# Routed experts moved ahead in layers 1 and 3 of a four-layer mixture kernel: sends over two stages, gathers beside other work

## The reference

```python
x = L0_attn_src
xn = _layernorm(x); s = _L0_attn_ref(xn, ...); g = _silu(_L0_ffn_ref(xn, ...)); x = x + s * g
xn = _layernorm(x); s = _L1_attn_ref(xn, ...); g = _silu(_L1_ffn_ref(xn, ...)); x = x + s * g
xn = _layernorm(x); s = _L2_attn_ref(xn, ...); g = _silu(_L2_ffn_ref(xn, ...)); x = x + s * g
xn = _layernorm(x); s = _L3_attn_ref(xn, ...); g = _silu(_L3_ffn_ref(xn, ...)); x = x + s * g
```

## Time and profile before

| what | value |
|---|---|
| median of three runs | 4465.07 us |
| lowest and highest | 4442.44 and 4473.7 us |
| the profiled execution's own time | 4474.3 us |
| its span, first to last instruction | 4472.5 us |
| busy in the span: PE, DVE, ACT, POOL | 3023.8, 2326.8, 1525.0, 813.9 us |
| mean granted TensorE clock | 0.822 |
| bytes moved by DMA | 150.88 MB, mean 34 GB/s |

### The profile page before, as it was taken

How to read it: one execution, slowest core, us unless ns; L and a number is a source line. 1 busy time by engine, 2 the same in 40 slices (tenths; PEclk the granted TensorE clock), 3 DMA queues, 4 the chain that set the end, 5 groups by cost and what they waited for, 6 DMA issues and landing times. The chain is left out here.

```text
span 4472.5 us, 65620 instructions
## 1 busy us (share of the span) xinstructions
PE 3023.8 (68%) x22266; PEld 2082.8 (47%) x22266; DVE 2326.8 (52%) x5222; ACT 1525.0 (34%) x2598; POOL 813.9 (18%) x800
## 2 busy tenths in 40 slices
PE   6999526999932314794346299999881537599990
PEld 4555414777720313442145145555571325476790
DVE  5555663111145463499553488888534468412443
ACT  4444112333322000000222188888531332243340
POOL 0000000000018301200134350000025564000015
PEclk9999757999956556897678599999995768699995
DMA  2000000000000022000034110000151000000471
GB/s 102 1 1 0 1 8 10 5 9 9 5 6 29 6 38 39 1 0 0 4 102 145 37 39 1 1 1 1 55 181 37 31 7 1 11 10 4 140 213 60
DMA packets 124861, 150.88 MB, mean 34 GB/s; under 512 B 50012, under 2 KB 95593, under 8 KB 124041
## 3 DMA queue, kind: packets, MB, share of 16 engines
q1 hardware_dynamic: 106584, 107.60, 8.7%
q0 software_dynamic: 18096, 41.06, 2.9%
HBM read 108.23 MB, written 40.37 MB: 33 GB/s over the span
## 5 line engine op out<-in xcount | busy, mean ns | idle before, releaser
L2183 DVE CUSTOM_DVE_ANT_0 decayed_sd<-decayed_sc,decayed_decay 128x512 f32<-128x512 f32 x512 | 331.7, 686 | 86.2 <-PE decayed_sc L2060 86.0
L2138 ACT ACTIVATE decayed_pr<-decayed_sd,decayed_shift 128x512 f32<-128x512 f32 x512 | 338.9, 713 | 49.5 <-DVE decayed_shift L2190 49.3
L668 PEld LDWEIGHTS experts_down<-experts_w,experts_h 128*128 128x128 f32 x2048 | 263.9, 192 | 107.1 <-issue 103.5
L2072 PEld LDWEIGHTS decayed_tr<-all_ident,decayed_pr 128*128 128x128 f32 x2048 | 223.5, 141 | 175.5 <-ACT decayed_pr L2138 101.7
L2072 PE MATMUL decayed_tr<-all_ident,decayed_pr 128*128 128x128 f32 x2048 | 276.9, 278 | 11.0 <-ACT decayed_pt L2145 10.8
L736 DVE SCALAR_TENSOR_TENSOR L0c_G<-experts_down,all_gate,L0c_G 128x128 f32 x256 | 85.5, 351 | 371.1 <-PE experts_down L668 371.1
L441 PE MATMUL experts_up<-experts_xt,experts_w 128*128 128x256 f32 x1140 | 272.0, 386 | 0.0
L702 ACT ACTIVATE experts_h<-experts_up,experts_w 128x512 f32<-128x512 f32 x256 | 175.9, 687 | 281.1 <-PE experts_up L657 279.7
L668 PE MATMUL experts_down<-experts_w,experts_h 128*128 128x128 f32 x2048 | 264.7, 275 | 0.0
L657 PE MATMUL experts_up<-all_XNT,experts_w 128*128 x512 | 258.7, 597 | 5.3 <-DMA experts_w<-in_L_experts 5.3
L198 PE MATMUL norm_turned<-all_ident,norm_xn 128*128 128x128 f32 x128 | 35.7, 434 | 299.6 <-DVE norm_xn L136 299.6
(11 more groups left out here) (468 smaller groups left out, 6377.1 us busy)
## 6 DMA issues: line engine op xcount, KB each, us to landing
experts_w<-in_L_experts SPq DMA_DIRECT2D x78, 384.0 KB, 3.4
experts_w<-in_L_experts SPq DMA_DIRECT2D x43, 579.0 KB, 4.0
experts_tok<-rows_in SPq DMA_DIRECT2D x121, 128.0 KB, 3.4
rows_out<-experts_y POOLq DMA_DIRECT2D x121, 128.0 KB, 3.4
rows_in<-linear_zero SPq DMA_DIRECT2D x43, 128.0 KB, 1.8
experts_w<-in_L_experts SPq DMA_DIRECT2D x8, 514.0 KB, 3.4
experts_b<-in_L_experts_b SPq DMA_DIRECT2D x43, 64.0 KB, 4.2
moe_w<-in_L_moe SPq DMA_DIRECT2D x4, 514.0 KB, 3.5
```

Source lines behind the costliest of these rows:

```text
L668: last = pe.matmul(down[b % 2][:, t * P:(t + 1) * P], h[:, b % 2, f, t * P:(t + 1) * P], w2, start=(f == 0 and t == 0), stop=(f == nf - 1) ...
L2072: last = pe.transpose(tr[u % TURNED][:, t * P:(t + 1) * P], pr[:, u % RING, t * P:(t + 1) * P], m.ident[:, :])
L2138: act.activation(pr[:, u % RING, :], sd[:, u % RING, :], ACT.Exp, bias=shift[:, u % RING:u % RING + 1]).then_inc(exp_ready, 1)
L2183: dve.tensor_tensor_reduce(out=sd[:, u % RING, :], in0=sc[h][:, :], in1=decay[:, qt, :], scale=1.0, scalar=-3.0e38, op0=ALU.mult, op1=ALU. ...
```

## The change

In layer 1 the sends of tiles 0 to 17 stay in the short convolution, and those of tiles 18 to 31 are issued in part b of the solve, which ends GpSimd's stream with the wait for all of them. `m.T` is no longer a spare buffer, since it must live longer; the solve gets a buffer of its own, which ends with the scan. Routed experts 1 run right after the scan. Their 64 gathers are issued by GpSimd in the statistics phase, where ScalarE now squares in place; the mix of branches uses `m.XNT` as its spare. The mix of layer 1 starts without gathers of its own.

In layer 3 `conv_project_phase` issues 3 tiles of sends per block in place of 4 and no longer waits for them; `rotate_phase` issues the last 8 tiles, one per block, its loop on GpSimd being written out, and waits for all. Routed experts 3 run right after the gated output projection. Their gathers are issued in the soft mixture `moe3`. Layer 2 keeps its order and its gathers.

```diff
@@ expert_phase(..., pool_beside=None)
+        @block.gpsimd
+        def _(pool):
+            if pool_beside is not None:
+                pool_beside(pool)
@@
+def gather_rows(pool, m, rows, collected):
+
+    for n in range(NB):
+        for t in range(n * TPB, (n + 1) * TPB):
+            for k in range(2):
+                pool.indirect_dma_start(rows[k][:, t, :], None, m.rows_out, bass.IndirectOffsetOnAxis(m.SLOT[:, k, t:t + 1], 0)).then_inc(collected[n], 16)
@@ collect_mix_phase
-            for n in range(NB):
-                for t in range(n * TPB, (n + 1) * TPB):
-                    for k in range(2):
-                        pool.indirect_dma_start(...)
+            if gather:
+                gather_rows(pool, m, rows, collected)
@@ short_conv_phase, and the same stream added to part b of solve_phase
-            for t in range(NT):
-                send_tile(pool, m, t, sent)
-            pool.wait_ge(sent, 2 * NT * 16)
+            send(pool)
@@ branch_stats_phase
+        squared = centred
+
+        @block.gpsimd
+        def _(pool):
+            gather(pool)
@@ conv_project_phase
-                for t in range(n * TPB, (n + 1) * TPB):
+                for t in range(n * 3, n * 3 + 3):
                     send_tile(pool, m, t, sent)
-            pool.wait_ge(sent, 2 * NT * 16)
@@ rotate_phase
-            with pool.Fori(0, NB) as n:
+            for n in range(NB):
                 pool.wait_ge(r_ready, n + 1)
                 pool.tensor_tensor(half[2][:, :, :, :], side(n, 0), spread(sin), ALU.mult)
                 pool.tensor_tensor(half[3][:, :, :, :], side(n, 1), spread(cos), ALU.mult).then_inc(mult, 1)
+                send_tile(pool, m, 3 * NB + n, sent)
+            pool.wait_ge(sent, 2 * NT * 16)
@@ build_layers, layer 1
+            def send1(first, end):
+                def issue(pool):
+                    for t in range(first, end):
+                        send_tile(pool, m, t, sent1)
+                    if end == NT:
+                        pool.wait_ge(sent1, 2 * NT * 16)
+                return issue
-            short_conv_phase(nc, "conv", m, d, b[0:3], sent1)
+            short_conv_phase(nc, "conv", m, d, b[0:3], send1(0, 18))
-            solve_phase(nc, "solve", m, k, beta, b[5], solved)
-            delta_scan_phase(nc, "scan", m, q, k, kc, vc, solved, beta, flat_s)
+            with Scope(nc, "L1solved") as inner:
+                solved = inner.sb("solved", [P, NT * P])
+                solve_phase(nc, "solve", m, k, beta, b[5], solved, send1(18, NT))
+                delta_scan_phase(nc, "scan", m, q, k, kc, vc, solved, beta, flat_s)
+            routed_phase(nc, "experts1", ...)
             fir_phase(nc, "fir", m, d, vc, b[2], (b[0], b[5]), b[1], b[3])
+            rows1 = (m.T, a.sb("rows", [P, NT, P]))
-            branch_stats_phase(nc, "stats", m, branches, b[5], b[6], b[0], b[2])
+            branch_stats_phase(nc, "stats", m, branches, b[5], b[0], b[2], lambda pool: gather_rows(pool, m, rows1, collected1))
-            mix_branches_phase(nc, "branches", m, d, b[5], branches, (b[6], b[2]), b[0])
+            mix_branches_phase(nc, "branches", m, d, b[5], branches, (m.XNT, b[2]), b[0])
-            routed_phase(nc, "experts1", ...)
-            collect_mix_phase(nc, "mix1", m, a.sb("rows", [P, 2, NT, P]))
+            collect_mix_phase(nc, "mix1", m, rows1, collected1)
@@ build_layers, layer 3
-            rotate_phase(nc, "rotate", m, d, qkv)
+            rotate_phase(nc, "rotate", m, d, qkv, sent3)
+            routed_phase(nc, "experts3", ...)     # now ahead of norm3a, soft3, moebias3, moe3, shared3
-            expert_phase(nc, "moe3", ...)
+            expert_phase(nc, "moe3", ..., pool_beside=lambda pool: gather_rows(pool, m, rows3, collected3))
-            routed_phase(nc, "experts3", ...)
-            collect_mix_phase(nc, "mix3", m, a.sb("rows", [P, 2, NT, P]), m.G)
+            collect_mix_phase(nc, "mix3", m, rows3, collected3, m.G)
```

More of the change, by code:

```diff
@@ L597, in _, with expert_phase @@
                     ins.then_inc(summed_free, 1)
-def expert_phase(nc, phase, m, n_experts, nf, kind, weights, acc, xt, bias=False, first=None, act_fn=None, gate=True):
+def expert_phase(nc, phase, m, n_experts, nf, kind, weights, acc, xt, bias=False, first=None, act_fn=None, gate=True, pool_beside=None):
     E = n_experts
@@ L789, in _, with collect_mix_phase @@
                     dve.tensor_tensor(flat(m.X, n), flat(m.X, n), sg[:, k, :], ALU.add).then_inc(sg_free, 1)
-def collect_mix_phase(nc, phase, m, rows, shared=None):
+def gather_rows(pool, m, rows, collected):
[3 more added lines that the diff above has]
+                pool.indirect_dma_start(rows[k][:, t, :], None, m.rows_out, bass.IndirectOffsetOnAxis(m.SLOT[:, k, t:t + 1], 0)).then_inc(collected[n], 16)
+def collect_mix_phase(nc, phase, m, rows, collected, shared=None, gather=False):
     with Scope(nc, phase) as s:
         g = s.sb("g", [P, 2, 512])
-        collected = [s.sem(f"collected{n}") for n in range(NB)]
         step, g_ready, sg_ready, mixed, done = map(s.sem, ("step", "g_ready", "sg_ready", "mixed", "done"))
@@ L821, in weigh @@
                 dve.wait_ge(collected[n], 2 * TPB * 16)
[L822 to L823 removed]
+                link(dve.tensor_tensor(rows[0][:, tiles, :], rows[0][:, tiles, :], share(0), ALU.mult))
+                link(dve.tensor_tensor(rows[1][:, tiles, :], rows[1][:, tiles, :], share(1), ALU.mult))
                 if shared is not None:
[L825 removed]
+                    link(dve.tensor_tensor(rows[0][:, tiles, :], rows[0][:, tiles, :], shared[:, tiles, :], ALU.add))
                 if n >= 2:
                     dve.wait_ge(mixed, n - 1)
[L828 removed]
+                dve.tensor_tensor(g[:, n % 2, :].rearrange("p (t d) -> p t d", d=P), rows[0][:, tiles, :], rows[1][:, tiles, :], ALU.add).then_inc(g_ready, 1)
             def add(n):
@@ L1279, in _, with short_conv_phase @@
             dve.tensor_copy(beta[:, :], by_chunk(turned[:, :])[:, :, 0]).then_inc(turn_done, 1)
-def short_conv_phase(nc, phase, m, d, outs, sent):
+def short_conv_phase(nc, phase, m, d, outs, send):
     TAPS = 4
@@ L1401, in _, with solve_phase @@
             link(dve.transpose(vc[:, :], v[:, :]))
-def solve_phase(nc, phase, m, k, beta, products, lanes):
+def solve_phase(nc, phase, m, k, beta, products, lanes, send):
     a_dram = nc.dram_tensor(f"{phase}_a", (P, NBC, 32), F32, kind="Internal").ap()
@@ L1706, in _, with branch_stats_phase @@
             dve.transpose(fs[:, :], fir[1][:, :]).then_inc(tap_done, 1)
-def branch_stats_phase(nc, phase, m, branches, centred, squared, stats, stats_t):
+def branch_stats_phase(nc, phase, m, branches, centred, stats, stats_t, gather):
     with Scope(nc, phase) as s:
@@ L2352, in _, with rotate_phase @@
             gate_logits(NB - 1)
-def rotate_phase(nc, phase, m, d, qkv):
+def rotate_phase(nc, phase, m, d, qkv, sent):
     PAIRS = 4
@@ L2568, in build_layers @@
             sent1 = a.sem("sent")
+            collected1 = [a.sem(f"collected{n}") for n in range(NB)]
+            def send1(first, end):
[5 more added lines that the diff above has]
+                return issue
             layer_norm_phase(nc, "norm1", m, m.X, m.XNT, m.T, router=d["L1_router"], n_experts=8)
@@ L2571, in build_layers @@
             b = [a.sb(f"b{n}", [P, NT * P]) for n in range(6)]
-            b.append(m.T[:, :, :].rearrange("p t d -> p (t d)"))
             beta = a.sb("beta", [P, NBC])
@@ L2602, in build_layers @@
         with Scope(nc, "L2c") as a:
-            collect_mix_phase(nc, "mix2", m, a.sb("rows", [P, 2, NT, P]))
+            rows2 = [a.sb(f"rows{k}", [P, NT, P]) for k in range(2)]
+            collect_mix_phase(nc, "mix2", m, rows2, [a.sem(f"collected{n}") for n in range(NB)], gather=True)
         m.router_bias = bias3[:, :]
@@ L2622, in build_layers @@
             m.GATE = a.sb("soft_gate", [P, NT, 4])
+            rows3 = [a.sb(f"rows{k}", [P, NT, P]) for k in range(2)]
+            m.G = a.sb("G", [P, NT, P])
+            collected3 = [a.sem(f"collected{n}") for n in range(NB)]
+            routed_phase(nc, "experts3", m, 12, 3, "glu", d["L3_experts"], down_bias=d["L3_experts_b2"], act_fn=ACT.Gelu, bias=True, sent=sent3)
             load_all(nc, "L3rows", [(rows[:, k, :], wide(x, P)) for k, x in enumerate(("L3_ln_g", "L3_ln_b"))])
```

17 lines of the change are left out of this document (4 added, 13 removed).

## The result

The changed kernel takes 4317.1 us, the median of four runs (4292.48 to 4327.72), beside 4454.72 for four runs of the kernel before on the same chip: a ratio of 0.968 (0.962 to 0.9739), 137.6 us less. The two profiled executions differ by 163.3 us: 4311.01 (span 4308.9) after, 4474.3 before. A stage runs here from its first instruction to that of the next (for the rotation its first product, 2.7 us behind its first load). One execution of the kernel before, of 8598.9 us, among the eleven that ran beside the last four experiments, is left out of their ratios.

What follows compares the result with a forecast made beforehand. No one engine bounds the kernel: each stage starts when every engine has left the one before. Layer 1 -74.8 and layer 3 -62.0, together -137, taken from 4465.07 give 4328 us; range 4290 to 4385.

Steps and rivals of the forecast that it cites:

- Short convolution: Layer 1's convolution: 28 sends fewer behind the last tap, and no wait for landing, -37.1 us.
- -23 for a pair without a stall: Short convolution: gain of only 23 us if no send stands still, since DVE's end then bounds the stage.
- The sign of "33 us": Profile check: the stage after the convolution starts 33 us after its last tap.
- Solve: Layer 1's solve: 28 sends run beside DVE's chain, plus a little for a fetch sharing DMA engines, +2 us.
- Statistics: 64 gathers beside the statistics: waits at four two-input DVE instructions, 15 us, plus GpSimd's exit, 5.6; +20.5 us.
- Rival 1: Statistics: gathers starve beside DVE, +71 us there, total 4378; chance 0.14.
- Rival 2: Statistics: gathers pass the four DVE products without waiting, total 4313; chance 0.12.
- Rival 3: Statistics: DVE is the one slowed, 28 us over four instructions, total 4356; chance 0.05.
- The mixes: Mixes of layers 1 and 3: gathers gone, DVE's instructions alone remain, -58.2 and -55.5 us.
- Projection: Layer 3's projection: 6 sends a block, GpSimd's beat falls from 11.06 to 8.53 us, -21.5 us.
- Rotation: Layer 3's rotation: two sends a block overfill GpSimd's idle time, 10.4 us, plus a tail of 4; +15 us.
- Experts 1: Layer 1's routed experts in their new place after the scan: a better clock start, -2 us.

Runs made afterwards that it cites:

- the last four experiments: The changed kernel again, it with linked scalings in the short convolution, and two further kernels, each timed in five rounds: 4315.48, 4298.03, 4271.56 and 4259.69 us.
- experiment 9: The changed kernel itself, unedited, timed again in five rounds: 4315.48 us, ratio 0.9648 to the kernel before.
- experiment 1: The changed kernel with all 64 sends of layer 1 in the solve and none in the short convolution: 4291.98 us.
- Experiment 7: The changed kernel with all 64 sends of layer 3 in the projection, 8 a block, and none in the rotation: 4340.85 us.
- experiment 11: The changed kernel with all layer 1 sends in the solve and its gathers split between statistics and gate network: 4271.56 us, ratio 0.9546.
- experiment 12: experiment 11 with layer 3's sends spread over projection, rotation and causal attention (its last eight tiles): 4259.69 us, ratio 0.9524.

## Why the prediction was right, step by step

**Short convolution, -37.1 forecast, -45.7 measured.** The mechanism was right, a stalled send included, the size off by three counts. The stall began 6.1 us later than in the earlier trace rows, so 17 sends went ahead, not 13: 4 x 1.273 = 5.1. GpSimd's exit after its last send was 1425.16 - 1421.86 = 3.3 us, not 5.6: 2.3. The stall's end came 1.1 us earlier. Together 8.5, against 8.6 found. Its other value, -23 for a pair without a stall, has no measurement, since the only profile of before has the stall; without one the changed stage takes 66.50 (experiment 9). That the profiled execution had a stall to match the forecast was luck: the same program can run without it. The sign of "33 us" from the last tap to the next stage does not fit the prediction's own sum, which makes 36 (72.82 less 37.1); 28.4 were found.

**Solve, +2 forecast, +1.8 measured: the number agrees by luck.** The prediction gave 2 us to the sends. They cost next to nothing, 64 of them in experiment 1 too: from the chain's first product to the scan it is 129.9 us, 129.4 before. Most of the 1.8 us lies ahead of the chain, and a clearing of semaphores moved there from the scan, which lost 2.2; the prediction had allowed 0 to 2 for one, as an addition.

**Statistics, +20.5 forecast, +21.6 measured: right by its own working.** It had 15 us for the four subtractions (15.7 found) and 5.6 for the exit (2260.94 - 2255.42 = 5.5). Rival 1, starvation, was ruled out in this stage. Rival 2, gathers that pass, fell with four gathers of 4.8 to 5.1 us. The Trainium skill (SBUF — State Buffer, "Who interferes with whom") infers that tensor_tensor would not stall a send: the four gathers, and eleven sends of 1.9 to 4.14 us in experiment 1's solve, contradict it. Its other sentence, that a tensor_reduce never contends, the trace bears out: 0.95 to 0.97 us beside reductions of 3 to 4.4 us. Rival 3 would have had DVE slowed: the subtraction kept its 4.42 us.

**The mixes, -58.2 and -55.5 forecast, -60.2 and -56.4 measured: right.** Of the 2 us more in mix 1, 1.3 are Silu's table load, which now lies beside DVE's first products and not ahead of them; the rest is the pitch, taken as 0.70 us where 40 instructions in 27.4 us make 0.685. The soft mixture covered all 64 gathers, as said.

**Projection, -21.5 forecast, -21.4 measured: right in sum, and its tail a little off.** The timeline of the changed kernel there, and in the rotation:

```profile
3461.39 1.05 POOL L2291 TENSOR_TENSOR project_delta<-project_x 128x512 f32<-128x512 f32 x1
...
3470.25 1.05 POOL L2291 TENSOR_TENSOR project_delta<-project_x 128x512 f32<-128x512 f32 x1
...
3510.35 1.17 POOL L2391 TENSOR_TENSOR rotate_half<-L3a_qkv,rotate_sin 128x512 f32<-128x512 f32 x1
...
3511.49 1.48 POOL L2392 TENSOR_TENSOR rotate_half<-L3a_qkv,rotate_cos 128x512 f32<-128x512 f32 x1
...
3513.13 1.27 POOL L367 DMA_INDIRECT rows_in<-L3a_at,all_slot  x1 [0.16 <-issue]
...
3514.71 1.10 POOL L367 DMA_INDIRECT rows_in<-L3a_at,all_slot  x1 [0.30 <-issue]
...
3515.83 1.19 POOL L2391 TENSOR_TENSOR rotate_half<-L3a_qkv,rotate_sin 128x512 f32<-128x512 f32 x1
```

(The prediction's 1.04 + 8 x 1.265 less a gap of 0.30 makes 10.86 and not the 11.06 of the rows; its sum used the rows.) This beat between deltas is 8.86 us (8.87 on average), not 8.53, mostly as one of the six sends takes 1.23 beside DVE's two-input instructions. TensorE's idle for delta is 2.45 us, not under 0.6, because GpSimd is still the bound in a shorter beat. The exit gave it back: the last send ends at 3487.43, the next stage's first load starts at 3491.65, 4.2 us for a forecast of 5.6.

**Rotation, +15 forecast, +0.6 measured: the term that failed.** The prediction set two sends of 2.5 us against 2.35 us of idle GpSimd and added a wait for DVE's dense instructions and a tail of 4. None came. Two beats in a row are 5.48 and 5.67 us; before, beats of 5.50 and 5.66 took turns in the same way. Only the first two beats are longer, 5.36 and 4.95 against 4.67 and 4.51. The sends delay GpSimd's first product until DVE is almost through with the last instruction of the block, and the product then takes 1.17 us in place of 1.85: the change made room for itself. The two sends keep to 1.27 and 1.10 us here, since 0.4 and 0.3 us are left of the DVE instructions that they start in, and to 1.27 and 1.26 in the next beat. So the step that failed is the overlap: it added the sends to GpSimd's products as long as they had been, and the first of them shrank by 0.7 us a block. And the stage's end has no exit of 5.6: the last send ends at 3538.11, DVE at 3540.56, and the next stage begins at 3541.22. Experiment 7 confirms the price at 0.7.

**Experts 1, -2 forecast, -0.2 measured**: no clock gain came. The output projection and experts 3 of layer 3 gave 2.2 where 0 was forecast; no run was made on that.

**The sum.** The prediction took 137 off the first median, 4465.07, and got 4328; 4317.1 was measured, within the range. The profiled pair shows -163.3, 26 more than the terms: 14.4 from the rotation, 8.6 from the convolution, 2.2 from the projection and experts of layer 3, and small ones. That the medians differ by just 137.6 is partly luck: the profiled run of before stands 19.6 us above the median of its kernel here, that of the changed kernel 6.1 below.

## What to carry to other kernels

Put GpSimd's DMA issues where GpSimd idles and DVE runs reductions or rests, and count each one that starts inside a two-input DVE instruction as ending 0.84 us behind that instruction; split them so that GpSimd ends before the engine that bounds the stage. When GpSimd is pushed later, price its own arithmetic again, since it may fall out of DVE's way or into it. Where a kernel's times scatter, compare stages of profiles, and look whether a repeating stage of one engine stands to another's stream in a way that a few hundredths of a microsecond decide.

## What the runs showed of the hardware

- **The exit of a block is paid per DMA.** From the end of GpSimd's last issue to the next stage: 5.5 us after 64 gathers, 4.2 after 48 sends, 3.3 after 36 (1421.86 to 1425.16). The prediction had a flat 5.6, from a stage with 64. From these three, some 0.08 us for each, as an estimate. The traces have GpSimd's drain at the end of a block by itself: 5.28 us after 64, 2.34 after the 28 of the solve, 1.35 after the 16 of the rotation, where DVE's end hides it.
- **A stalled send of 42 to 49 us** that depends on a position between engines, in six of the eight profiles with unlinked taps, and moves the stage from 66.5 to 92.6 or 98.9 us. It would account for most of the 36 us over which the changed kernel scatters.
- **A DVE product waits for a GpSimd product that is already running, and the causal attention has two lengths by it.** It takes 141.31 us in the changed kernel and 149.63 in experiment 11, with the same instructions (141 to 143 in six profiles, 149 to 150 in seven). The table of stretches, first of the changed kernel, then of experiment 11, has DVE busy 8 us longer, and 13 us idle in both:

```profile
3541.00:3682.00 141.00, 114.12 (x448) 87.53 (x448) 127.92 (x68) 36.20 (x32) 89.83 (x64) 0.90 0.00 0
```

```profile
3492.00:3641.00 149.00, 113.90 (x448) 84.96 (x448) 135.91 (x68) 36.20 (x32) 97.24 (x64) 0.92 0.00 0
```

The groups of instructions of that stage hold the difference in one line, DVE's product (busy us, mean ns, idle before it and what ended it). It is shown for the changed kernel, experiment 11 and experiment 12:

```profile
L2519 DVE TENSOR_TENSOR causal_weighed<-causal_sums,L3a_qkv 128x1152 f32<-128x1152 f32 x32 | 51.1, 1598 | 8.2 <-ACT causal_sums L2507 8.2
```

```profile
L2523 DVE TENSOR_TENSOR causal_weighed<-causal_sums,L3a_qkv 128x1152 f32<-128x1152 f32 x32 | 59.7, 1867 | 8.2 <-ACT causal_sums L2511 8.2
```

```profile
L2530 DVE TENSOR_TENSOR causal_weighed<-causal_sums,L3a_qkv 128x1152 f32<-128x1152 f32 x32 | 67.4, 2105 | 7.4 <-ACT causal_sums L2518 7.4
```

Of the 96 products in these three profiles 51 take 1.33 to 1.38 us. The other 45 take 1.56 to 4.52, and each of them starts while a product of GpSimd is running; only one of the 51 does, with 0.13 us left. A product that begins first keeps its 1.35 us. What sets the two streams one way or the other from run to run was not tested.
